# Sliding-window attention and ternary FFN on one core: the window mask folded into all score passes, a second masked query tile, b2 added by GpSimd

## The reference, cut to what matters

```python
x = x + attn(layernorm(x), Wq, Wk, Wv, Wo)      # 16 heads of 16, scale 1/4
x = x + ffn(layernorm(x), W1, b1, W2, b2)       # W1, W2 quantized to -1/0/1, relu between
# in attn: allowed = (j <= i) & (j > i - 64); softmax(q @ k.T * scale + bias) @ v
# in ffn:  out = relu(x @ W1q.T + b1) @ W2q.T + b2
```

## Time and profile before

| what | value |
| --- | --- |
| median of 3 runs | 691.57 us (691.31 to 692.96) |
| the profiled execution: its time, its span | 696.39 us, 694.6 us |
| PE busy | 653.9 us, 94% |
| DVE, ACT, POOL busy | 611.0, 567.7, 556.4 us |
| mean granted TensorE clock | 0.980 |
| transfers | 314433 packets, 70.59 MB |

### The profile page before, as it was taken

How to read it: one execution, slowest core, us unless ns; L and a number is a source line. 1 busy time by engine, 2 the same in 40 slices (tenths; PEclk the granted TensorE clock), 3 DMA queues, 4 the chain that set the end, 5 groups by cost and what they waited for, 6 DMA issues and landing times.

```text
span 694.6 us, 23901 instructions
## 1 busy us (share of the span) xinstructions
PE 653.9 (94%) x8048; PEld 557.4 (80%) x8048; DVE 611.0 (88%) x1391; ACT 567.7 (82%) x2489; POOL 556.4 (80%) x823
## 2 busy tenths in 40 slices
PE   7668789999999999999999999999999999998888
PEld 5446578888888888888878898888888888887776
DVE  4879889898999989899998999899899989897854
ACT  5588788898998988898988988898898988796622
POOL 7367899888888979888887989888898978887831
PEclk9889899999999999999999999999999999999999
DMA  8555563746465654736465564746465463643110
GB/s 291 77 104 114 90 111 62 142 81 114 78 130 96 132 98 92 134 78 118 85 132 96 115 117 90 123 82 122 85 131 98 90 114 58 122 81 78 32 39 31
DMA packets 314433, 70.59 MB, mean 102 GB/s; under 512 B 283076, under 2 KB 305862, under 8 KB 314312
## 3 DMA queue, kind: packets, MB, share of 16 engines
q1 hardware_dynamic: 281848, 42.43, 38.7%
q10 hardware_dynamic: 32464, 26.63, 13.2%
HBM read 20.25 MB, written 9.44 MB: 43 GB/s over the span
## 4 chain that ended last, share of the span: by engine, by line
PE 69%; SPq 7%; POOL 6%; DVE 6%; DMA 5%; ACT 4%; issue 3%; ACTq 0%; POOLq 0%; DVEq 0%
PE ps L1101 14%; PE ps L1089 11%; PE ps L1000 10%; PE ps L980 9%; PE ps L1037 8%; PE ps L1062 6%; PE ps L1048 4%; SPq L284 4%; DMA k<-kst 3%; SPq L304 3%; POOL tl L419 2%; PE ps L973 2%; PE ps L1074 2%; ACT p L523 2%; PE ps L1026 2%
## 5 line engine op out<-in xcount | busy, mean ns | idle before, releaser
L523 ACT ACTIVATE p<-ps,negm 128x96 f32<-128x96 f32 x1024 | 335.0, 355 | 16.9 <-DVE negm L724 16.3
L419 POOL TENSOR_TENSOR tl<-pt,th 128x384 f16<-128x384 f32 x256 | 234.4, 916 | 20.7
L523 ACT ACTIVATION_READ_ACCUMULATOR p<-ps,negm 128x1 f32 x1024 | 228.1, 223 | 0.0
L724 DVE TENSOR_REDUCE negm<-ps 128x4 f32<-128x384 f32 x256 | 138.2, 540 | 39.3 <-PE ps L980 36.3
L417 POOL CAST th<-pt 128x384 f16<-128x384 f32 x256 | 128.8, 503 | 32.0 <-DVE pt L741 31.8
L741 DVE STREAM_TRANSPOSE pt<-p 128x384 f32<-128x384 f32 x256 | 143.5, 561 | 3.0 <-ACT p L523 2.9
L980 PE MATMUL ps<-k,qbd 128*128 128x96 f16 x1536 | 125.6, 207 | 0.0
L980 PEld LDWEIGHTS ps<-k,qbd 128*128 128x128 f16 x1536 | 106.1, 99 | 11.1 <-issue 0.3
L1000 PE MATMUL ps<-th,vb 128*128 128x96 f16 (+1 forms) x1120 | 100.5, 205 | 2.2 <-DVE osum L800 1.6
L1000 PE MATMUL ps<-tl,vb 128*128 128x96 f16 (+1 forms) x1120 | 100.5, 205 | 0.0
L1000 PEld LDWEIGHTS ps<-th,vb 128*128 128x128 f16 x1120 | 96.4, 115 | 2.8 <-issue 1.7
(11 more groups left out here) (141 smaller groups left out, 1430.7 us busy)
## 6 DMA issues: line engine op xcount, KB each, us to landing
k<-kst SPq DMA_DIRECT2D x32, 288.0 KB, 4.0
vb<-vd SPq DMA_DIRECT2D x256, 32.0 KB, 2.0
rwide<-parked ACTq DMA_DIRECT2D x32, 256.0 KB
out<-x ACTq DMA_DIRECT2D x32, 256.0 KB, 3.7
qbd<-qs SPq DMA_DIRECT2D x254, 32.0 KB, 2.8
x<-in_L_attn_hidden ACTq DMA_DIRECT2D x15, 512.0 KB, 4.5
kw<-kst SPq DMA_DIRECT2D x31, 192.0 KB, 4.4
k<-kst SPq DMA_DIRECT2D x31, 144.0 KB, 3.8
```

The source lines that it names most:

```text
L419: e.tensor_tensor(tl[g % 2][:, o], pt[n % 3][:, :], th[g % 2][:, o], ALU.subtract).then_inc(s_lo, 1)
L523: ins = e.activation(p[:, 96 * u:96 * u + 96], bank[:, 96 * u:96 * u + 96], ACT.Exp, bias=m[:, u:u + 1], accum_out=r[:, u:u + 1])
L724: e.tensor_reduce(negm[n % 4][:, :], sbank[n % 3][:, 0:384].rearrange("p (a b) -> p a b", b=96), AX.X, ALU.max, negate=True).then_inc(s_mx, 1)
```

## The change

- **Scores.** `qm` and `kw` are there for all four groups; pass 1 always uses them, and the mask matmul of L973 is gone. The full mask of the first slots stays. Column counts of the two passes are as before.
- **Transfers.** The upper queries take 12 transfers rather than 8 (24 a chunk with the lower ones), the upper keys 4 rather than 2 (for each group a plain one of 144 KB and one into `kw` of 192 KB, instead of one of 288 KB).
- **Head.** ScalarE fills four `kw` tiles rather than two, GpSimd two `qm` tiles rather than one.
- **b2.** It is loaded once as a 128 x 256 tile and added to x by GpSimd (`add_b2`, after `c_norm`); the matmul of L1096 is gone, and VectorE's last `residual` waits for the addition (`s_b2`).
- **Slots.** Some steps move by one or two slots.

```diff
-V_LATE = 10
-A_T, A_Q, A_K, A_V = (1, 2), (5, 14), (6, 15), (10, 13)
+V_LATE = 9
+A_T, A_Q, A_K, A_V = (1, 2), (6, 14), (6, 15), (10, 13)
-Q_DMA, K_DMA, V_DMA, A_CARRY = (7, 20), (15, 22), 17, 1
+Q_DMA, K_DMA, V_DMA, A_CARRY = (7, 20), (15, 22), 18, 2
+C_B2 = (13, 18)
-PV_LAG, O_ADD, O_SPLIT = 8, 9, 15
+PV_LAG, O_ADD, O_SPLIT = 8, 9, 14
-W_ABS, W_TERNARY, W_FOLD = (1, 2, 3, 4), (6, 8, 10, 12, 14, 16, 18, 20), (15, 16, 17, 18, 19, 20)
+W_ABS, W_TERNARY, W_FOLD = (0, 1, 2, 3), (6, 8, 10, 12, 14, 16, 18, 20), (15, 16, 17, 18, 19, 20)
...
-                if t:
-                    e.dma_start(ks[g][:, :, :].rearrange("p m n -> p (m n)"),
-                                bass.AP(tensor=src, offset=row, ap=[[2 * w, 64], [0, 2], [1, 2 * w]])).then_inc(d_k[g], 16)
-                else:
-                    e.dma_start(ks[g][:, 0, :], bass.AP(tensor=src, offset=row, ap=[[2 * w, 64], [0, 2], [1, w]])
-                                ).then_inc(d_k[g], 16)
-                    e.dma_start(bass.AP(tensor=kw[g][:, :, :].tensor, offset=0, ap=[[2 * 1536, 64], [1, 1536]]),
-                                bass.AP(tensor=src, offset=row + w, ap=[[2 * w, 64], [32, 16], [1, 96]])).then_inc(d_k[g], 16)
+                e.dma_start(ks[g][:, :], bass.AP(tensor=src, offset=row, ap=[[2 * w, 64], [0, 2], [1, w]])
+                            ).then_inc(d_k[g], 16)
+                e.dma_start(bass.AP(tensor=kw[g][:, :, :].tensor, offset=0, ap=[[2 * 1536, 64], [1, 1536]]),
+                            bass.AP(tensor=src, offset=row + w, ap=[[2 * w, 64], [32, 16], [1, 96]])).then_inc(d_k[g], 16)
...
-            for (to, v), hs in zip(((qbd[t], 0), (qm, 0), (qbd[t], 1)), heads):
-                if to is qm and t == 1:
-                    continue
+            for (to, v), hs in zip(((qbd[t], 0), (qm[t], 0), (qbd[t], 1)), heads):
...
+            def add_b2(h):
+                c, u = divmod(h, 2)
+                e.wait_ge(s_xnC, h + 1)
+                if h == 0:
+                    e.wait_ge(d_b2, 16)
+                x2 = xs[c % NX][:, 2 * u:2 * u + 2, :]
+                e.tensor_tensor(x2, x2, b2w[:, :, :].to_broadcast([128, 2, D]), ALU.add).then_inc(s_b2, 1)
...
-                for g in range(2):
+                for g in range(4):
                     e.activation(kw[g][:, :, :], kmask.unsqueeze(1).to_broadcast([128, 16, 96]), ACT.Copy).then_inc(s_kw, 1)
...
+                if name[0] == "y":
+                    e.wait_ge(s_b2, 2 * c + u + 1)
...
-                elif g >= 2:
-                    ends = bank[:, 0:384].rearrange("p (u j k) -> p u j k", j=3, k=32)[:, :, 0:3:2, :]
-                    seen = maskf[:, 288:384].rearrange("p (j k) -> p j k", k=32)[:, 0:3:2, :]
-                    e.matmul(ends, identb[:, :], seen.unsqueeze(1).to_broadcast([128, 4, 2, 32]), start=True, stop=False,
-                             skip_group_check=True)
...
-                e.matmul(bank[:, o], ones[:, 0:128], bp[:, F:], start=True, stop=False)
```

More of the change, by code:

```diff
@@ L149, in build @@
         identh = sb("identh", [128, 128], f16)
[L150 removed]
+        bp = sb("bp", [128, F], f16)
         xs = [sb(f"x{i}", [128, 4, D], f32) for i in range(NX)]
@@ L171, in build @@
         qbd = [sb(f"qbd{t}", [128, 2, 16 * 128], f16) for t in range(2)]
-        qm = sb("qm", [128, 2, 16 * 128], f16)
-        ks = [sb(f"k{g}", [128, 1 + g // 2, 64 + CH], f16) for g in range(4)]
-        kw = [sb(f"kw{g}", [128, 16, 96], f16) for g in range(2)]
+        qm = [sb(f"qm{t}", [128, 2, 16 * 128], f16) for t in range(2)]
+        ks = [sb(f"k{g}", [128, 64 + CH], f16) for g in range(4)]
+        kw = [sb(f"kw{g}", [128, 16, 96], f16) for g in range(4)]
         vd = sb("vd", [128, 4, 2, 4, 16, 4], f16)
@@ L189, in build @@
         hT = [sb(f"hT{p}", [128, 8, CH // 2], f16) for p in "hl"]
+        b2w = sb("b2w", [128, 1, D], f32)
         gpart = sb("gpart", [128, 2, 2], f32)
@@ L217, in build @@
         s_const, s_wlo, s_fc = sem("s_const"), sem("s_wlo"), sem("s_fc")
-        s_xn0 = sem("s_xn0")
+        s_xn0, s_b2, d_b2 = sem("s_xn0"), sem("s_b2"), sem("d_b2")
         s_gs, s_thr, s_tb, s_td = sem("s_gs"), sem("s_thr"), sem("s_tb"), sem("s_td")
@@ L236, in build @@
         smask, kmask = pr[0][:, 0:64].bitcast(f16), pr[0][:, 64:112].bitcast(f16)
-        bt = (hT[0][:, :, :].rearrange("p a b -> p (a b)").bitcast(f32), hT[1][:, 0:2, :].rearrange("p a b -> p (a b)").bitcast(f32))
+        bt = hT[0][:, :, :].rearrange("p a b -> p (a b)").bitcast(f32)
         below = hT[1][:, 4:8, :].rearrange("p a b -> p (a b)").bitcast(f32)
@@ L255, in place_k @@
                 e.wait_ge(s_zk, 1)
-                e.wait_ge(s_kw, 2)
+                e.wait_ge(s_kw, 4)
             for g in (2 * t + i for i in groups):
@@ L276, in place_q @@
                 e.wait_ge(s_zq, 1)
-            for (to, v), hs in zip(((qbd[t], 0), (qm, 0), (qbd[t], 1)), heads):
-                if to is qm and t == 1:
-                    continue
-                if to is qm and c == 0:
-                    e.wait_ge(s_zm, 1)
+            for (to, v), hs in zip(((qbd[t], 0), (qm[t], 0), (qbd[t], 1)), heads):
+                if to is qm[t] and c == 0:
+                    e.wait_ge(s_zm, t + 1)
                 e.wait_ge((s_ahi, s_alo)[v], 8 * c + 3 + 4 * t)
@@ L348, in mask_queries @@
                 e.wait_ge(d_s, 16)
-                e.tensor_copy(qm[:, :, :].rearrange("p g j -> p (g j)").bitcast(f32).rearrange("p (b j) -> p b j", j=64),
-                              pr[0][:, 0:64].unsqueeze(1).to_broadcast([128, 32, 64])).then_inc(s_zm, 1)
+                for t in range(2):
+                    e.tensor_copy(qm[t][:, :, :].rearrange("p g j -> p (g j)").bitcast(f32).rearrange("p (b j) -> p b j", j=64),
+                                  pr[0][:, 0:64].unsqueeze(1).to_broadcast([128, 32, 64])).then_inc(s_zm, 1)
             def carry(c):
@@ L365, in biases @@
             def biases():
-                e.wait_ge(d_b, 64)
-                e.tensor_copy(bp[:, 0:F], bt[0][:, :])
-                e.tensor_copy(bp[:, F:], bt[1][:, :]).then_inc(s_bh, 1)
+                e.wait_ge(d_b, 32)
+                e.tensor_copy(bp[:, :], bt[:, :]).then_inc(s_bh, 1)
             def rstd_a(c):
@@ L450, in _ @@
                     low(n - L_PART)
+                for u in range(2):
+                    c = stage_c(n, C_B2[u])
+                    if c is not None:
+                        add_b2(2 * c + u)
                 ct = pair_at(n, R_MUL)
@@ L977, in scores @@
                     for m in range(2):
-                        to = qm if g < 2 and m else qbd[g // 2]
-                        keys = kw[g][:, blk, :] if g < 2 and m else ks[g][:, m, 32 * blk:32 * blk + 96]
+                        to = qm[g // 2] if m else qbd[g // 2]
+                        keys = kw[g][:, blk, :] if m else ks[g][:, 32 * blk:32 * blk + 96]
                         ins = e.matmul(bank[:, 96 * u:96 * u + 96], to[:, g % 2, 128 * blk:128 * blk + 128], keys,
-                                       start=(g < 2 and not first and m == 0 and u == 0),
+                                       start=(not first and m == 0 and u == 0),
                                        stop=(m == 1 and u == 3), skip_group_check=True)
@@ L1101, in c_y @@
                         ins = e.matmul(bank[:, o], hT[hp][:, f, t * 128:(t + 1) * 128], w2T[:, f, :],
-                                       start=False, stop=(f == 7 and hp == 1))
+                                       start=(f == 0 and hp == 0), stop=(f == 7 and hp == 1))
                 if t:
```

32 lines of the change are left out of this document (15 added, 17 removed).

## The result

| what | before | after |
| --- | --- | --- |
| median | 692.27 us (691.31 to 693.03, 4 runs) | 757.74 us (751.63 to 758.27, 4 runs) |
| the profiled execution: its time, its span | 696.39 us, 694.6 us | 751.63 us, 749.8 us |
| mean granted TensorE clock there | 0.980 | 0.947 |

The ratio is 1.0926, 95% interval 1.0868 to 1.0985. The forecast was 762.5 us, in a range of 722 to 790. The profiled execution after is the shortest of its four; the others had mean clocks of 0.934 to 0.937, so the trace shows a little less lost clock than the median holds.

The account below looks back on a forecast made before the run. Two paths critical at once, SP's V to slot 8 and PE's slot 8 to V. From 696.4: head +6, SP's half +56.3, PE's half with clock +10, tail -1.5 give 767.2; as median 762.5 us, range 722 to 790.

Parts of the forecast that it names:

- Two halves of one loop: Middle chunks: SP's path from V to slot 8 (22.0 us) and PE's from slot 8 to V (17.0) make the period.
- Q1 to K1: SP's query issues between V and slot 8: twelve for eight take 9.05 us against 6.4, +2.7 a chunk.
- The landing of kw2: End of SP's path to slot 8: kw2 lands in 4.4 us against 4.0, +0.4, behind one more issue of +0.65.
- PE's half: Slot 8 to the next V: seven masks and two biases fewer, 1.0 us saved, from 17.0 to 16.05.
- Clock, 1.7 a chunk: PE behind its 4.2 us wait at slot 8: the half clock costs 1.7 us a chunk, bounds 0 and 2.6.
- The clock stays up: Rival, chance 0.25: waits of 4 us at slot 8 but no clock loss on PE's work; 738.7 us.
- Head, +6: Start of the kernel: more kw fills and six more issues ahead of V of chunk 0, +6 us, bounds 2 and 9.
- GpSimd, 0: b2 additions on GpSimd, 2.5 us a chunk, fit its period at 84%: nothing is paid.
- The queue has room: Rival, chance 0.05: all 30 issues under 0.58 us keep SP's path under PE's 21.7 us; faster, 674 us.
- Slots: nothing, 1 us either way: Steps changing places ahead of slot 8's wait: no effect on time, 1 us either way.
- More than a sum: Rival, chance 0.07: extra packets slow issues and landings, +5.4 rather than 3.75, half clock costs 2.6; 800 us.
- GpSimd takes over: Rival, chance 0.03: with SP's path short, GpSimd holds the period at about 39; 692 us, no change.

Follow-up runs that it names:

- e9: Changed kernel without the four upper qm and the kw2, kw3 transfers from the second chunk on: 685.72 us, 0.9936 of the kernel before.
- e1: Kernel before plus only the change's six extra transfers on SP, into tiles nobody reads, the key ones waited for by the scores: 778.49 us, ratio 1.122.
- e4: Changed kernel with 45 extra 128-column matmuls on PE ahead of its wait in slot 8, from the third chunk on: 752.53 us, ratio 1.0856.
- e5: Changed kernel with the two value products two slots sooner, A_V from (10, 13) to (8, 11): 725.23 us, ratio 1.0463.
- e10: Changed kernel without the four upper qm transfers from the second chunk on, kw2 and kw3 kept: 699.54 us, ratio 1.0132.
- e2: Changed kernel with the six extra transfers of each chunk from the second on issued by ScalarE's queue in slot 4: 719.1 us, ratio 1.0352.

## Why the prediction was right, step by step

- **Two halves of one loop.** Right, and the strongest evidence is e9 beside e1: each half moves while the other keeps its length but for the clock, and the period is their sum. They aren't wholly independent: in e4 and e5 SP's half grew by 0.9 and 1.5 us though none of its transfers was changed.
- **Q1 to K1: 9.1 us.** Measured 9.17. Twelve issues with the gaps between them, as the rows of the lower queries had it.
- **The landing of kw2: +0.4 on the old 4.0, with an issue of +0.65 in front.** This term was mis-sized. The transfers of the kernel after (KB each, us to landing) are:

```profile
kw<-kst SPq DMA_DIRECT2D x63, 192.0 KB, 3.8
k<-kst SPq DMA_DIRECT2D x63, 144.0 KB, 3.5
...
qm<-qs SPq DMA_DIRECT2D x128, 32.0 KB, 2.4
```

  The 4.4 was that of `kw0` and `kw1` behind twelve lower queries. In the kernel after all land sooner, in the median; that the k transfer ahead of kw2 is half as large fits this and e1, and isn't shown by itself. K1 to slot 8 is 4.41 rather than 5.05, V to slot 8 25.1 rather than 25.85. Over 15 chunks that is 11 us of the sum.
- **PE's half, -1.0.** Where the clock stayed up slot 8 to V took 16.35 us, 0.66 less rather than 1.0; e9 and e10 show the same. The traces say where the rest is. PE's second value product and VectorE's split behind it, which releases V, before (slot 8 at 399.52) and after (slot 8 at 429.53):

```profile
413.22 0.38 PE L1048 MATMUL ps<-wvh,xTAh 128*128 128x256 f16 x2
415.85 0.67 DVE L792 SCALAR_TENSOR_TENSOR vd<-ps,vd 128x512 f16<-128x512 f32 x1
...
442.36 0.38 PE L1051 MATMUL ps<-wvh,xTAh 128*128 128x256 f16 x2
445.17 0.67 DVE L798 SCALAR_TENSOR_TENSOR vd<-ps,vd 128x512 f16<-128x512 f32 x1
```

  The product stands 12.83 us behind slot 8 rather than 13.70, 0.87 sooner, which is eight matmuls of 0.11: the seventh mask, that of slot 14, comes behind the product and not ahead of it. The split gained only 0.7 of this (15.64 for 16.33), as VectorE had other work between.
- **Clock, 1.7 a chunk.** The size is right, the number of times was not. PE in the 8 us behind its waits (length, PE busy, clock, DMA), behind waits of 3.32, 3.70, 3.47, 2.85, 3.89, 4.16 and 3.63 us in that order:

```profile
177.10:185.10 8.00, 8.00 (x112) 1.00 0.54 69
262.90:270.90 8.00, 8.00 (x97) 0.79 0.56 75
305.90:313.90 8.00, 8.00 (x100) 0.83 0.59 76
429.60:437.60 8.00, 8.00 (x112) 1.00 0.64 95
512.20:520.20 8.00, 8.00 (x96) 0.79 0.58 75
600.40:608.40 8.00, 8.00 (x90) 0.68 0.56 67
644.00:652.00 8.00, 7.74 (x80) 0.63 0.59 73
```

  A mean of 0.79 over 8 us of dense work is 1.7 us lost, just the row that was taken; 0.68 is 2.6, the upper bound that was named, and 0.63 a little more. But in 6 of the 13 middle chunks nothing was lost, so the mean is 1.0 us. "The clock stays up", then, held for less than half of the chunks, and the forecast for the rest. The other runs of the kernel were 6 to 7 us longer with mean clocks 0.010 to 0.013 lower; if all of that fell behind slot 8, their mean is about 1.5 a chunk, an estimate, and the term was nearly right for them.
- **Head, +6.** V of chunk 1 starts at 70.03 us rather than 63.84: +6.2. V of chunk 0 ended at 56.78 (forecast 55.3), and the first value product waited 6.0 us for it.

```profile
44.11 12.67 SPq L300 DMA_DIRECT2D vb<-vd  x16
...
70.03 5.58 SPq L300 DMA_DIRECT2D vb<-vd  x8
58.26 0.24 PE L1003 MATMUL ps<-th,vb 128*128 128x96 f16 x1 [5.99 <-issue]
```

  But the table of slots by itself brings V of chunk 1 forward by 3.5 us, so, if the two add up, the transfers and fills are worth 9.7 of the head, over the upper bound of 9 for it, and "Slots: nothing, 1 us either way" was wrong by 3.5. The two misses cancel in a right sum.
- **GpSimd, 0.** Right: one addition takes the 1268 ns that were taken from L391, its busy time rose by 39.6 us, and b2 alone gives 0.9992.

```profile
L412 POOL TENSOR_TENSOR x<-x,b2w 128x512 f32<-128x512 f32 x32 | 40.6, 1268 | 0.2
```

- **The queue has room.** The point named for it, under 0.58 us for each of 30 issues, wasn't met: V to K1 is 28 issues in 20.7 us, 0.74 each. The Trainium skill, "DMA: Bandwidth & Descriptors", "Issuing engines are not separate DMA queues", calls this time usually small relative to the transfer. Here a query issue of 0.66 us (2.65 for four) stands beside 2.4 us to landing, a quarter of it; the issues add up and the landings overlap. By e9 and e10 the five make V to slot 8 3.2 us longer.
- **More than a sum, GpSimd takes over.** The extra packets didn't slow the issues (V to Q1 is 11.5 us as before), so the first has nothing to stand on in the kernel after. For the second e9 gives a hint of where it would decide: with SP's path short, GpSimd is on the chain for 28% of the span, at a period of 38.3.
- **Sum.** In the profiled executions the loss was 55.2 us against a forecast of 70.8: about 11 too much for the landings and 10 for the clock, and 4 to 5 the other way for PE's smaller gain. In the medians it was 65.5; the forecast took 4.8 off for the execution of before, while that of after lay 6 under its own median. So part of the closeness of 757.7 to 762.5 is these two differences, not the working.

## What to carry to other kernels

Before work is moved from the engine that is busy for all of the time to a queue, look for the loop in which both stand: where a queue's chain of issues and the busy engine arrive together, an issue of 0.6 to 0.7 us on the one costs more than the 0.11 us matmuls it saves on the other. A queue with 5 us idle in each period has no slack if that idle time lies ahead of the step that opens the loop. Starting that step earlier pays only by what really moves: two slots in the table were 2.5 us of slot 8 to V and one slot 0.2, and SP's half grew by 1.5 us when it started two slots sooner. Split such a change by its parts: the transfers alone (+12%), all but the transfers (-0.6%), the slots alone (-0.6%) said at once what the whole, +9%, didn't.

## What the hardware showed that was not expected

- The granted clock after a wait is not given by the wait's length: in the kernel after waits at slot 8 of 2.85 to 3.32 us were followed by 1.00 and those of 3.47 us and more by 0.63 to 0.83 over the next 8 us, while the kernel before shows 0.72 over 6 us behind one of 2.80, and the one with `A_V` (9, 12) 0.79 over 8 us behind one of 2.57 and 1.00 behind one of 2.73.
- The same transfers on the same queue took 0.9 us longer from V to slot 8 when PE was given 45 small matmuls in its wait (26.0 against 25.1), and why stays open.
- How soon the keys land depends on how close the issues ahead of them stand. In e10, in the chunks in which PE waited for kw2, K1 to slot 8 was 4.3 to 4.6 us where Q1 to K1 had taken 7.1 to 7.6, and 4.7 to 5.9 where it had taken 5.4 to 6.5. A faster chain of issues was in part given back by the landing.
- An issue on ScalarE's queue holds ScalarE's activations: in e2 six in a row made a gap of 4.57 us there.
